# Two of eight key tiles of P V in three fp16 products, with their remainders on VectorE

## The reference

```
q, k, v = x @ Wq, ctx @ Wk, ctx @ Wv          # 16 heads of 64
logits = einsum('bhqd,bhkd->bhqk', q, k) * 64**-0.5 + col_bias
probs = softmax(logits)
out = einsum('bhqk,bhkd->bhqd', probs, v) @ Wo + bo + x
```

## Time and profile before

| | |
|---|---|
| median of 3 runs | 3498.78 us |
| the profiled execution | 3498.58 us, span 3496.4 us |
| TensorE matmul busy | 3364.5 us (96% of the span) |
| VectorE busy | 2350.3 us (67%) |
| GpSimd busy | 2183.0 us (62%) |
| ScalarE busy | 1766.3 us (51%) |
| granted TensorE clock, mean | 0.993 |

### The profile page before, as it was taken

One profiled execution on the slowest core, in us unless ns is written; L12 is line 12 of the kernel. 1 busy time (PEld: TensorE's weight loads), 2 busy tenths in 40 slices (PEclk: granted clock), 3 DMA queues, 4 the chain that ended last, 5 costly groups with the idle time before them and its releaser, 6 DMA issues.

```text
span 3496.4 us, 70163 instructions
## 1 busy us (share of the span) xinstructions
PE 3364.5 (96%) x27442; PEld 1544.6 (44%) x27442; DVE 2350.3 (67%) x4444; ACT 1766.3 (51%) x2230; POOL 2183.0 (62%) x1050
## 2 busy tenths in 40 slices
PE   6999999999997888889999999999999999999998
PEld 3444444444442322234444444444444444444443
DVE  5666666666656788856676666666666666666666
ACT  4444444444445677764444444444444444444444
POOL 4877777777650000028777777777787677767776
PEclk8999999999999999999999999999999999999999
DMA  4000000000000000000000000000000000000000
GB/s 145 10 10 10 1 10 10 9 3 9 6 10 11 8 12 17 17 1 10 10 1 10 10 10 1 10 10 9 3 10 10 1 10 10 10 1 10 3 1 25
DMA packets 50178, 42.10 MB, mean 12 GB/s; under 512 B 4928, under 2 KB 42176, under 8 KB 49856
## 3 DMA queue, kind: packets, MB, share of 16 engines
q1 hardware_dynamic: 49136, 37.08, 3.5%
q10 hardware_dynamic: 720, 0.53, 0.1%
HBM read 32.36 MB, written 2.10 MB: 10 GB/s over the span
## 4 chain that ended last, share of the span: by engine, by line
PE 90%; ACT 3%; DVE 3%; POOL 2%; issue 2%; DMA 0%; SPq 0%; ACTq 0%; POOLq 0%; DVEq 0%
PE ps_j L863 39%; PE ps_j L1052 19%; PE ps_st L1012 13%; PE ps_sm L946 6%; PE ps_st L997 3%; PE ps_j L1039 3%; ACT pt L1473 2%; PE ps_sm L1026 2%; POOL acc L719 2%; PE ps_j L1072 1%; PE ps_st L946 1%; PE ps_j L955 1%; PE ps_j L1088 0%; PE ps_j L1063 0%; DVE nmg L1893 0%
## 5 line engine op out<-in xcount | busy, mean ns | idle before, releaser
L719 POOL TENSOR_TENSOR acc<-acc,pt 128x1024 f32<-128x1024 f32 x570 | 1365.3, 2395 | 438.9 <-ACT pt L1473 384.8
L1473 ACT ACTIVATE pt<-ps_st 128x1024 f32<-128x1024 f32 x768 | 743.0, 1019 | 447.0 <-PE ps_st L1012 435.2
L1052 PE MATMUL ps_j<-pt,v 128*64 128x512 f32 x3040 | 694.2, 598 | 1.4 <-DVE q_l L1808 1.3
L1903 DVE CUSTOM_DVE_ANT_0 ps_sm<-ps_sm,bias_m,nmx 128x512 f32<-128x512 f32 x666 | 480.3, 757 | 272.6 <-PE ps_j L946 227.6
L863 PE MATMUL ps_j<-w_h,ctx_h 128*128 128x128 f16 x3072 | 532.6, 220 | 1.6 <-ACT rinv L1489 1.1
L863 PE MATMUL ps_j<-w_l,ctx_h 128*128 128x128 f16 x3072 | 531.5, 219 | 0.0
L863 PE MATMUL ps_j<-w_h,ctx_l 128*128 128x128 f16 x3072 | 531.4, 219 | 0.0
L1903 DVE CUSTOM_DVE_ANT_0 ps_sm<-ps_sm,bias_m 128x512 f32<-128x512 f32 x486 | 334.5, 706 | 197.1 <-PE ps_j L946 186.4
L740 POOL TENSOR_TENSOR o_un<-o_un,rinv 128x512 f32<-128x512 f32 x111 | 142.0, 1280 | 477.2 <-ACT rinv L1485 294.9
L1052 PEld LDWEIGHTS ps_j<-pt,v 128*64 128x64 f32 x3040 | 201.7, 136 | 407.6 <-issue 369.6
L1940 DVE RECIPROCAL rinv<-rinv 128x256 f32<-128x256 f32 x190 | 331.3, 1746 | 14.0 <-ACT rinv L1489 4.5
(11 more groups left out here) (186 smaller groups left out, 5483.0 us busy)
## 6 DMA issues: line engine op xcount, KB each, us to landing
w_raw<-wk SPq DMA_DIRECT2D x25, 256.0 KB, 2.7
pt<-ctx_t SPq DMA_DIRECT2D x6, 1024.0 KB, 7.8
w_raw<-wv SPq DMA_DIRECT2D x24, 256.0 KB, 3.7
wo_raw<-wo SPq DMA_DIRECT2D x28, 128.0 KB, 2.0
w_raw<-wq SPq DMA_DIRECT2D x24, 128.0 KB, 2.8
k_h<-k_l SPq DMA_DIRECT2D x72, 32.0 KB, 1.9
x<-x_t SPq DMA_DIRECT2D x4, 512.0 KB, 8.9
acc<-ctx_t SPq DMA_DIRECT2D x2, 1024.0 KB, 8.1
```

What stands on the lines that cost most here:

```text
L719: G.tensor_tensor(total, first, pt[:, n % RING, :], ALU.add).then_inc(s_acc, 1)
L1052: last = MM(dst[h * HD:(h + 1) * HD, :], values_of(p)[:, kt, h * HD:(h + 1) * HD], pt[:, (units(p) + kt) % RING, h * TQ:(h + 1) * TQ], sta ...
L1473: A(pt[:, n % RING, :], src.rearrange("p h q -> p (h q)"), ACT.Exp).then_inc(s_exp, 1)
L1903: last = V.tensor_tensor_reduce(out=src, in0=src, in1=bias_m[:, t, half * HALF:(half + 1) * HALF], scale=-1.0, scalar=nmx[:, 0, t, h:h + 1 ...
```

## The change

For items whose own slot and both neighbouring slots are `turned` (items 1 to 27 and 49 to 109), key tiles 2 and 3 of P V, in `attend(s, 0)`, are computed as three fp16 products. The values of these two tiles are rounded by ScalarE (`values_hi`) and their remainder is taken by VectorE (`values_lo`), both in the slot before; both parts lie in the space of the fp32 values. The exponentials of these tiles are written two places further in the ring; ScalarE rounds them (`probs_hi`) into the tile's own place and VectorE subtracts (`probs_lo`) into the other half of that place. All exponentials of wide items carry a factor of 1024, by a bias, which cancels in the division by the sum. `take` waits for the value remainder too before the bank of `v0` is used again.

In the order of the slot: ScalarE puts the two roundings behind the query split and behind the first key half, and `values_hi` ahead of `values(s + 1, 0)`. VectorE puts the first subtraction between `queries_lo` and `keys_lo(s + 2, 0)`, the second behind the second reciprocal and ahead of `keys_lo(s + 2, 1)`, and `values_lo` between the opening and closing maxima of block 2.

Moved besides: in layer 1 the remainders of the next weights and output weights go from VectorE to GpSimd (each as a scaling and a subtraction). Ahead of item 0 the remainder of x goes from GpSimd to VectorE, and that of context piece 3 the other way.

```diff
@@ in take @@
                     elif before in ("v0", "v1"):
                         pe.wait_ge(s_v_sb, values_before(m) + 1 + int(before[1]))
+                        if in_terms(m) and before == "v0":
+                            pe.wait_ge(s_v_l, terms_before(m) + 1)
@@ in attend @@
                     kt = part * 4 + k
+                    if parted(p, kt):
+                        n = terms_before(p)
+                        pe.wait_ge(s_v_l, n + 1)
+                        pe.wait_ge(s_p_l, 2 * n + k - 1)
+                        (vh, vl), (ph, pl) = value_parts(p), parts(p, kt)
+                        for i, (v, q) in enumerate(((vh, ph), (vh, pl), (vl, ph))):
+                            for h in range(2):
+                                last = MM(dst[h * HD:(h + 1) * HD, :], v[:, k - 2, h * HD:(h + 1) * HD],
+                                          q[:, h * TQ:(h + 1) * TQ], start=False, stop=k == 3 and i == 2)
+                        continue
@@ ScalarE @@
+            def values_hi(p):
+
+                act.wait_ge(s_v, values_before(p) + 1)
...
+                A(value_parts(p)[0], bank("v0", p)[:, 2 * P:4 * P].rearrange("p (k d) -> p k d", k=2), ACT.Copy,
+                  scale=VS / WS)
+
...
+            def probs_hi(p, j):
+                act.wait_ge(s_exp, units(p) + j + 1)
+                place_free(units(p) + j)
+                A(parts(p, j)[0], whole(p, j), ACT.Copy).then_inc(s_p_h, 1)
@@ ScalarE's turned_slot @@
                     queries_hi(s + 2)
-                    if not splits_x(s):
-                        keys_hi(s + 2, 0)
+                if termed:
+                    probs_hi(s, 2)
+                if far and not splits_x(s):
+                    keys_hi(s + 2, 0)
+                if termed:
+                    probs_hi(s, 3)
+                if far:
                     keys_hi(s + 2, 1)
                 if past:
                     output_hi(s - 1)
+                if nxt and in_terms(s + 1):
+                    values_hi(s + 1)
                 if nxt:
                     values(s + 1, 0)
@@ VectorE @@
+            def values_lo(p):
+                dve.wait_ge(s_v_sb, values_before(p) + 1)
+                hi, lo = value_parts(p)
+                split_lo(lo, bank("v0", p)[:, 2 * P:4 * P].rearrange("p (k d) -> p k d", k=2), VS / WS, hi
+                         ).then_inc(s_v_l, 1)
+
+            def probs_lo(p, j):
+                dve.wait_ge(s_p_h, 2 * terms_before(p) + j - 1)
+                hi, lo = parts(p, j)
+                V.tensor_tensor(lo, whole(p, j), hi, ALU.subtract).then_inc(s_p_l, 1)
@@ VectorE's turned_slot @@
                     queries_lo(s + 2)
-                    if not splits_x(s):
-                        keys_lo(s + 2, 0)
+                if in_terms(s):
+                    probs_lo(s, 2)
+                if far and not splits_x(s):
+                    keys_lo(s + 2, 0)
                 if past and not grouped(s - 1):
                     reciprocal(s - 1, 1)
+                if in_terms(s):
+                    probs_lo(s, 3)
                 if far:
                     keys_lo(s + 2, 1)
                 peak()
+                if nxt and in_terms(s + 1):
+                    values_lo(s + 1)
                 peak()
@@ GpSimd's loop @@
                 if s == -2:
-                    pool.wait_ge(s_ext_k, 1)
-                    split_x_lo(0, 0)
+                    pool.wait_ge(s_init, 1)
                     context_lo(2)
+                    context_lo(3)
                 elif s == -1:
-                    split_x_lo(0, 1)
...
+                if grouped(s) and s % B == 0:
+                    weights_lo(set_of(s) + 1)
+                    wo_lo(set_of(s))
```

## The result

| | before | after |
|---|---|---|
| median of the runs, us | 3498.55 (3498.06 to 3499.04) | 3618.59 (3617.26 to 3619.4) |
| span of the profiled execution, us | 3496.4 | 3615.1 |
| steady slot, from one first key product to the next, us | 30.03 | 31.20 |
| mean granted clock | 0.993 | 0.992 |

The ratio is 1.0342, with a 95% interval of 1.033 to 1.0354: 3.4% slower. The forecast was 3580, from 3530 to 3650.

The account below looks back on a forecast made before the run. TensorE, busy 96% of the span, was taken as the bound. 88 items at +0.95 us gave +84; 3496.4 + 84 - 3 - 2 + 2 = 3577.4, plus 2.2 around the span: 3580 us, range 3530 to 3650.

Parts of the forecast that it names:

- P V: Two key tiles as three fp16 products each instead of fp32: saves 0.42 us per item, 37 us over 88 items.
- this case alone: The main forecast, VectorE and GpSimd taking turns, without the rivals: 3580 us, from 3535 to 3620; chance 0.78.
- First remainder: probs_lo(2), held by GpSimd's third addition, ends 1.08 us after it; TensorE stalls 0.62 us before project_v.
- Second remainder: probs_lo(3) starts ahead of normalize and delays keys_lo(1); TensorE's opening maxima come 0.20 us later still.
- GpSimd first: Rival: normalize gets in before probs_lo(3); +2.2 us per item, 3690 us, or 3620 to 3690 if partly; chance 0.09.
- Output product: Waits for output_lo and values_lo: 0.55 us more per item; 0.44 us late even with no hold by GpSimd.
- Bias: The bias log 1024 in the exponential: said to cost nothing that a row shows.
- Slots that split x: Six or so slots with GpSimd busier: +2 us, between -2 and +8.
- Ahead of item 0: Exchanged subtractions make TensorE's first query product wait less: 0 to -5 us, taken as -2.
- Layer 1: weights_lo and wo_lo go from VectorE to GpSimd at four slots: 0 to -6 us, taken as -3.
- No hold: Rival: remainders run beside GpSimd at 1.1 us, only values_lo stalls, 0.02 us per item; 3493 to 3500 us; chance 0.08.
- The whole gain: Rival: also values_lo gets in before the maxima or costs nothing; 3459 us; chance 0.05.

Follow-up runs that it names:

- add3_late: Changed kernel with GpSimd's third addition moved behind normalize and output_lo: 3540.96 us, ratio 1.0123.
- add3_waits: Changed kernel with one wait more: GpSimd's third addition, still ahead of normalize, waits for the first probability remainder: 3523.32 us, ratio 1.0071.
- products_only: Changed kernel without the remainders of probabilities and values; all three products take the high parts: 3476.65 us, ratio 0.9938.
- side_back: Changed kernel with the moved work ahead of item 0 and in layer 1 put back on its engines: 3618.24 us, ratio 1.0343.
- best_less: best, but items whose own slot also splits x keep P V in fp32: 3464.02 us, ratio 0.9904.
- best: add3_waits with values_lo between the opening maxima's two heads, the factor as a constant in the maxima copy, work ahead of item 0 put back: 3478.87 us, ratio 0.9947.

## Why the prediction was right, and where it was off

**The mechanism was right.** Its steps against the slot above:

| step, us per item | forecast | measured |
|---|---|---|
| stall ahead of `project_v` (first remainder held) | 0.62 | 0.64 |
| stall ahead of the opening maxima | 0.20 | 0.32 |
| stall ahead of the output product | 0.55 | 0.50 |
| first key product waits on ScalarE | 0 | 0.14 |
| P V | -0.42 | -0.43 |
| sum | 0.95 | 1.17 |

By the table the forecast's steady slot was 0.22 short, 0.14 of it by the bias. For the whole kernel the sum was 38 us short (span 3615.1 against 3577.4; the measured time still lies just inside the 3535 to 3620 given for this case alone). Like for like these are 20 us in the 82 steady slots, 9 in slots 49 and 78 to 81, 5 up to the first output product, 2 in layer 1 with the steps beside it, and 1.5 in the last two. All five have the same sign, so none hid another.

The first three are differences of the distances between TensorE's starts: 5.82 from the first key product to `project_v`, then 3.42, then 2.33, where the earlier trace rows have 5.18, 3.10 and 1.83.

*First remainder.* Forecast to end 1.08 after the addition: it ended 1.08 after. That two orders of work which keep the pair apart make it 1.21 settles the cause. The Trainium skill, "SBUF — State Buffer", section "Who interferes with whom", says that a VectorE instruction with two SBUF inputs contends with a GpSimd instruction that reads SBUF, and that issue order decides which of them blocks; the trace agrees in both directions (3.06 against 1.21; `normalize` 2.12 against 1.27).

*Second remainder.* The order forecast (it gets in ahead of `normalize`) came true; the rival "GpSimd first" did not. The term was 0.12 short. From the first `k_l`'s end to the second's are 3.33 us (1998.54 to 2001.87), forecast 3.30; the other 0.09 is that `project_v` followed its `k_l` by 0.06 and the opening maxima theirs by 0.15, where I had put 0.15 for both.

*Output product.* `values_lo` ended 0.28 after the last piece of the maxima (2003.86 to 2004.14), as forecast, and `o_l` was last, as forecast: it ended at 2004.29, and the product started 0.06 later. That even with no hold `values_lo` would make this product 0.44 late was right too: add3_late and add3_waits show 0.42 (30.17 against 29.75).

*Bias.* The forecast said that the bias in the exponential costs "nothing that a row shows", and this was wrong. It costs 0.09 us in each exponential, and 0.14 an item where two stand ahead of the `rinv` copy; 12 of the 38 us by which the sum was short. The row of ScalarE's idle time was read, not the chain from its last exponential to TensorE. The Trainium skill, "ScalarE: Activation LUTs", section "What ACT_TABLE_LOAD costs", gives 93 ns for each pointer operand of an ACTIVATE; the rows here give 1110 - 1019 = 91 ns.

*Slots that split x.* The second mis-sized term. For slots 49 and 78 to 81 the forecast comes to 5 x 0.95 + 2 = 6.8 us, and they took 4.7 + 11.2 = 15.9. GpSimd's queue is full there, so a held instruction pushes `normalize` as well. In products_only slots 78 to 80 are each 0.3 faster than before and slot 81 is 0.2 slower, so nearly all of it is the remainders'.

*Ahead of item 0.* Forecast -2, measured +4.2. TensorE's first query product did come earlier (18.96 against 22.35), but a wait of 3.86 us for the first `k_l` took that back (a later block of maxima starts at 33.19 against 33.07), and by the next maxima it is 1.35 behind (41.34 against 39.99). In between, from 32 to 37 us, the granted clock was 0.51, where the kernel before had 0.66, and from 37 to 42 it was 0.80 against 1.00; that part is the clock's. Of the 4.2, side_back gives back 1.1, and products_only, which has no remainders, 2.3. best_less, which has the work put back and keeps item 1 in fp32, has its first output product at 114.00 against 113.79 before, and best, which up to there differs from it in item 1 only, at 116.49: there slot 1's three products cost 2.5. How the rest of the 4.2 divides between the moved work and the clock is open.

*Layer 1.* Forecast -3. Measured is -2.4 from item 33 to 46, for another reason: no gain of the moved work shows, and the profiled execution of the kernel before had stretches at a lower clock. So the near match is luck. At item 32 the changed kernel even lost 1.5 (its clock was 0.88 over that step, 0.93 before).

**The rivals.** "No hold" priced at 3493 to 3500 would have needed the remainders at 1.1 us. With the first remainder kept free by the wait (add3_waits) it comes out at 3523, higher because of the bias (12 us) and the slots that split x (11). "The whole gain", 3459, is what best_less nearly reaches, 3464, through what that rival asked for, `values_lo` inside the maxima, and with two edits more: the constant instead of the bias, and six items left in fp32. "GpSimd first" did not occur in the steady slots.

## What to carry to other kernels

Before two-input SBUF work is given to VectorE, lay its instructions beside GpSimd's in time: where they overlapped here, the one that started later took its own time on top of the rest of the other's, and everything queued behind it moved. One semaphore wait that makes GpSimd start after the VectorE instruction, in idle time it had anyway, was worth 95 us of 3619 here. A saving on the engine that bounds the kernel is only kept where each hand-over to it has room: list these hand-overs with their room (before the change the first `k_l` had 1.0 us, 5.55 to 6.62 in the earlier trace rows, the second 1.5, and the `rinv` copy about 0.18 - 0.14 = 0.04), and price every instruction that grows ahead of each.

## What the runs showed of the hardware

The exponential of 128x1024 takes 1019 ns without and 1108 to 1110 with a bias column; the same shift as a constant in the copy of the maxima cost nothing (629 ns either way, period 29.61). A held instruction of VectorE ended 1.08 us after the GpSimd instruction ended, against 1.16 to 1.21 unhindered: nothing of its work but some 0.1 us was done in the hold. And TensorE's granted clock fell to the 1.2 GHz level (0.50 from 1621.80 to 1623.40) within an idle of 1.96 us in one kernel and did not in idles of 1.82 and 0.43 us in another. Steps of 1 to 1.6 us in single slots that no edit explains should be looked up in the granted clock before they are given a cause, and medians that differ by a few us should be compared at equal mean clock.
